# Cross-attention with a mixture of experts: GpSimd's large operations placed behind each tile's low part and doubled copy

## The reference, cut to what matters

```python
# 16 batch items: x (16, 56, 256), context (16, 1500, 256); 16 heads of 128
q = rms_norm(x @ q_w + q_b, nq_s)
k_img, v_img = rms_norm(img @ ki_w + ki_b, nki_s), img @ vi_w + vi_b    # first 257 context rows
k_txt, v_txt = rms_norm(txt @ k_w + k_b, nkt_s), txt @ v_w + v_b        # the other 1243 rows
out = sdpa(q, k_txt, v_txt) + sdpa(q, k_img, v_img)                     # scale 1/sqrt(128)
x = x + out @ o_w + o_b          # x is normalised before q
...
# then 32 experts of which each token takes 4, and a shared one
x = x + ffn(layernorm(x))
```

## Time and profile before

| | us |
|---|---|
| median of three runs | 1808.75 |
| the profiled execution | 1808.77 |
| its span, first to last instruction | 1807.0 |
| attention loop within it, about | 231 to 1364 |
| busy in the whole span: PE, DVE, POOL, ACT | 1718.9, 1343.6, 1199.1, 983.1 |

### The profile page before, as it was taken

The page is one execution under the profiler, slowest core; times in us unless marked ns, Lnnn a source line. Parts: engine busy times, 40 slices in busy tenths (PEclk is TensorE's granted clock), DMA queues, the critical chain, the costliest instruction groups (busy, mean ns, idle before and its releaser), DMA issues. The chain is left out here.

```text
span 1807.0 us, 31191 instructions
## 1 busy us (share of the span) xinstructions
PE 1718.9 (95%) x8731; PEld 1540.5 (85%) x8731; DVE 1343.6 (74%) x2561; ACT 983.1 (54%) x1657; POOL 1199.1 (66%) x1053
## 2 busy tenths in 40 slices
PE   7899989999999999999999999999996997699998
PEld 6677779989889889889899898898885896588887
DVE  4444577887878878878878878778775783677776
ACT  3455546665665665656665656656645662344443
POOL 1233578889888898898898898888866420233332
PEclk8999989999999999999999999999998997899999
DMA  3276574466565665665564665656566960233332
GB/s 116 91 251 230 203 200 109 113 129 125 133 123 123 135 128 119 137 137 124 129 132 120 128 128 131 122 124 134 116 196 185 326 210 28 97 113 114 116 115 71
DMA packets 419413, 251.25 MB, mean 139 GB/s; under 512 B 352320, under 2 KB 370880, under 8 KB 417568
## 3 DMA queue, kind: packets, MB, share of 16 engines
q1 hardware_dynamic: 419360, 250.61, 54.1%
HBM read 187.71 MB, written 60.10 MB: 137 GB/s over the span
## 5 line engine op out<-in xcount | busy, mean ns | idle before, releaser
L1405 ACT ACTIVATE p_high<-psum,key_rms 128x448 fp32r<-128x448 f32 x384 | 245.0, 638 | 345.9 <-PE psum L1226 345.8
L1224 PE MATMUL psum<-u_high,c_high 128*128 128x448 f32 x768 | 284.2, 370 | 6.5 <-POOLq L1837 5.9
L1224 PE MATMUL psum<-p_high,c_high 128*128 128x448 f32 (+1 forms) x768 | 284.8, 371 | 4.9 <-DVE p_low L1488 4.9
L1225 PE MATMUL psum<-u_low,c_high 128*128 128x448 f32 x768 | 281.9, 367 | 0.0
L1226 PE MATMUL psum<-u_high,c_low 128*128 128x448 f32 x768 | 281.6, 367 | 0.0
L1226 PE MATMUL psum<-p_high,c_low 128*128 128x448 f32 (+1 forms) x768 | 280.9, 366 | 0.0
L1225 PE MATMUL psum<-p_low,c_high 128*128 128x448 f32 (+1 forms) x768 | 280.9, 366 | 0.0
L1499 DVE COPY psum<-beta_wide 128x448 f32<-128x448 f32 x416 | 259.3, 627 | 20.2 <-DMA beta_wide<-absorbed_biases 4.4
L1488 DVE TENSOR_TENSOR p_low<-psum,p_high 128x448 fp32r<-128x448 f32 x384 | 236.7, 616 | 45.3 <-ACT psum L1407 42.9
L1719 POOL TENSOR_TENSOR c_low<-stage,c_high 128x512 fp32r<-128x512 f32 x208 | 270.3, 1300 | 0.0
L1407 ACT ACTIVATE psum<-psum,key_rms 128x448 f32<-128x448 f32 x384 | 232.9, 606 | 0.0
(11 more groups left out here) (274 smaller groups left out, 4032.6 us busy)
## 6 DMA issues: line engine op xcount, KB each, us to landing
stage<-in_ctx SPq DMA_DIRECT2D x210, 256.0 KB, 2.7
averages<-o_raw SPq DMA_DIRECT2D x64, 448.0 KB, 5.2
u_raw<-absorbed_queries SPq DMA_DIRECT2D x60, 448.0 KB, 5.5
absorbed_queries<-u_stage SPq DMA_DIRECT2D x14, 1792.0 KB, 6.8
u_stage<-averages SPq DMA_DIRECT2D x20, 896.0 KB, 6.1
beta_wide<-absorbed_biases SPq DMA_DIRECT2D x32, 448.0 KB, 5.4
recip_wide<-reciprocals SPq DMA_DIRECT2D x32, 448.0 KB, 4.0
p_wide<-probs_by_expert SPq DMA_DIRECT2D x32, 448.0 KB, 3.5
```

What stands on the lines that cost most here:

```text
L1224: nc.tensor.matmul(out, high, rhigh, start=start, stop=False, **kw)
L1225: nc.tensor.matmul(out, high, rlow, start=False, stop=False, **kw)
L1405: nc.scalar.activation(p_high[:, probs_slot(u), :], src, ACT.Exp, scale=key_rms[:, t:t + 1])
```

## The change

`X` moves from each even step to the odd step behind it, where it stands behind S and T. ACT's high parts of the image rows move from steps 10 and 12 to 11 and 13. `split_lone` moves from steps 17 and 19 to 16 and 18, so that it stands behind K. In the first item the scaling of the second text half stays at step 0. Every instruction is the same as before.

```diff
-        TEXT_SPLIT, IMAGE_SPLIT = (1, 3), (10, 12)
-        LONE_TERMS, LONE_HIGH, LONE_LOW = (12, 14), (14, 16), (17, 19)
+        TEXT_SPLIT, IMAGE_SPLIT = (1, 3), (11, 13)
+        LONE_TERMS, LONE_HIGH, LONE_LOW = (12, 14), (14, 16), (16, 18)
...
-                    if step == 0 and has_prev:
+                    if step == 1 and has_prev:
                         scale_u(it, TEXT, 1)
                     if step == 0 and not has_prev:
                         scale_first(TEXT, 1)
...
-                    if step in (2, 4):
-                        split_u(it, TEXT, (step - 2) // 2)
-                    if has_next and step in (8, 10):
-                        scale_u(it + 1, IMAGE, (step - 8) // 2)
-                    if has_next and step in (12, 14):
-                        split_u(it + 1, IMAGE, (step - 12) // 2)
-                    if has_prev and step in (16, 18):
-                        scale_o(it - 1, TEXT, (step - 16) // 2)
-                    if step in (20, 22):
-                        scale_o(it, IMAGE, (step - 20) // 2)
-                    if has_next and step == 24:
+                    if step in (3, 5):
+                        split_u(it, TEXT, (step - 3) // 2)
+                    if has_next and step in (9, 11):
+                        scale_u(it + 1, IMAGE, (step - 9) // 2)
+                    if has_next and step in (13, 15):
+                        split_u(it + 1, IMAGE, (step - 13) // 2)
+                    if has_prev and step in (17, 19):
+                        scale_o(it - 1, TEXT, (step - 17) // 2)
+                    if step in (21, 23):
+                        scale_o(it, IMAGE, (step - 21) // 2)
+                    if has_next and step == 25:
                         scale_u(it + 1, TEXT, 0)
```

## The result

The changed kernel takes 1811.13 us (median of 15 runs, 1807.16 to 1814.88) against 1807.43 for the kernel before (15 runs on the same chips, 1802.39 to 1809.63). The ratio is 1.0023, with a 95% interval of 1.0013 to 1.0033: slower by about the 0.2% that can be told from no change. The profiled execution has a span of 1809.4 us, against 1807.0.

A forecast was written before the change was run, and what follows sets the result against it. PE was taken as the bound, busy 69.67 of each item's 70.22 us. Items 2 to 16 +3.0, first item +1.3, last item -2.1 sum to +2.2 on 1808.75: forecast 1811.0 us, range 1803.5 to 1821.5.

The forecast's parts named there:

- The new wait at unit 7: PE waits about 1.1 us per item for the text rows' second low part, 5.33 after the norm of step 4.
- Rival 3: Change doesn't reach PE: text low part out in time, item stays 70.22, total 1808.8; chance 0.16.
- The held cast: DVE's row-sum cast beside step 1's text scaling on GpSimd ends 0.26 us after it; norm of step 2 only 0.95 earlier.
- Rival 2: Faster: DVE's cast is not held and the first item's clock stays up, -8.2 us, 1800.6; chance 0.14.
- rival 1: DVE's gain dies between the norms of steps 1 and 4; each item pays +0.76, total 1821; chance 0.25.
- PE's gains: Next item's first scores no longer wait, -0.31 us; the second lone unit's seed wait shrinks as DVE's norms come earlier.
- Per item: Unit 7 starts +0.12 to +0.26 us later, +0.20 taken; bounds -0.30 and +0.76; items 2 to 16 give +3.0.
- The last item: DVE's wait for a small DMA behind output loads ends 3 us earlier, PE gains 2.1 us; bounds -2.1 and 0.
- The first item: PE keeps 0.3 of 1.6 us gained; the clock's fall moves before unit 7, costing 1.6: +1.3 in all.
- The sum: Whole kernel: 3.0 + 1.3 - 2.1 = +2.2 us, forecast 1811.0.
- rival 4: The new gap drops PE's clock in each item: 15 x 1.6 us more, total 1835; chance 0.05.

The follow-up runs named there:

- e1: The changed kernel with the text rows' low parts back at steps 2 and 4, before the tile's low part; 1795.39 us, ratio 0.9935.
- e4: The changed kernel with step 1's text scaling done on half its columns, the rest left unscaled; 1797.06 us in one run.
- e7: The kernel before, order untouched, with the lone low parts computed for only 64 of 448 columns; 1793.29 us in one run.
- e6: The kernel before with only the image rows' scaling, low parts and ACT's high parts moved; 1795.37 us, ratio 0.9932.
- e3: e1 with the text scaling also back at steps 24 and 0, so no text operation is moved; 1792.99 us, ratio 0.9922.
- e8: e3 with the text low part's first half at step 3, behind the doubled copy, second half still at step 4; 1791.78 us, ratio 0.991.

## Why the prediction was right, and where it was not

**The new wait at unit 7: right.** 5.33 us from the norm of step 4 was forecast, 5.25 measured, and the wait is there in all 16 items: 1.01 beyond the pace in a steady one (1.1 forecast), 1.90 in the first. e1 prices it at 0.97 an item. Rival 3, a low part that is out in time, falls on it.

**The held cast: right in the full profile** (0.26 behind the scaling's end forecast, 0.25 measured), and e4 prices it at 0.62 of the item. Rival 2, faster because the cast is not held, falls on this row. So does rival 1, a cast held until DVE's whole gain is gone: its item would have been 0.76 longer, not 0.27.

**PE's gains: right in place.** The seed's wait and the hidden 0.31 at the item's first scores are gone. A hidden 0.22 at unit 5, where the forecast had a seed's wait shrink, stayed.

**Per item:** +0.20 forecast, +0.27 measured, just past the working's own 0.12 to 0.26 and well inside its outer bounds.

**The last item: right.** From its first lone matmul to its last attention matmul it took 65.12 and takes 63.19: -1.93 (-2.1 forecast). The wait for the sums' DMA fell from 4.77 to:
```profile
1324.08 0.20 DVE L1585 RECIPROCAL recip_cols<-sum_cols 112x8 f32<-112x8 f32 x1 [1.01 <-DMA sum_cols<-sums]
```

**The first item was mis-sized: +1.3 forecast, +0.5 measured** (72.84 to 73.34). The mechanism was right. PE now stands 1.90 later on, at 252.86, and the clock falls behind it instead of behind the earlier gap. Windows of the changed kernel (us, then busy and count for PE, PEld, DVE, ACT, POOL, then the granted clock, DMA share, GB/s):
```profile
249.00:250.00 1.00, 1.00 (x7) 0.92 (x6) 0.94 (x2) 0.55 (x2) 0.95 (x1) 1.00 1.03 414
...
253.00:254.00 1.00, 1.00 (x5) 0.90 (x6) 0.98 (x2) 0.00 (x0) 1.00 (x2) 0.77 0.30 99
254.00:255.00 1.00, 1.00 (x4) 0.92 (x3) 0.63 (x1) 0.05 (x1) 0.92 (x2) 0.50 0.03 10
```
The working charged the fall anew with 1.6 and gave only 0.3 back, although the same stretch of half speed (1.2 GHz) had already stood in the item before the change. It moved; it was not added. e7, whose first item has a gap of 0.66 in place of the 1.89 and no stretch at half speed, gives its price: the item is 2.74 shorter there, 1.23 of it by the gap, which leaves 1.5 for the clock. So the 1.6 was about the right size, but it was already in the 72.84.

**The sum.** To the output stage's first matmul (at 1370.33 before and 1373.98 now) the change costs 3.65: the prologue 0.6, the first item 0.5, fourteen items 4.46, the last -1.93. Of the fourteen, item 2 alone is 0.75 (69.73 to 70.48, below), the others 0.28 or 0.29 on the mean. Against the forecast's terms that is 0.6 and 1.46 more for the prologue and the items, 0.8 less for the first, 0.17 less given back in the last. The stages behind gave back 1.2, which no run explains, so the span grew by 2.4 against 2.2 forecast, and the median of many runs by 3.7. The near hit of the span is in part errors that cancel.

**What the reading missed,** though it did not spoil the sum, is what the stall was. The prediction took each wait of DVE's norm as the work of the X that stands in that pair. It was one lag: 0.86 were there when the averages' stretch began (e6 takes these away), two rounds that hold a lone low part and an averages' scaling made 1.60 of it, and it was carried over the item's end. The trace of before held the counterexample: item 1 has no text averages to scale at steps 16 and 18, its norms of the last steps have no wait,
```profile
279.90 0.43 DVE L1513 CUSTOM_DVE_ANT_0 junk<-psum,c_twice 128x257 bf16<-128x257 f32 x1 [0.56 <-POOL c_twice L1732]
...
284.85 0.43 DVE L1513 CUSTOM_DVE_ANT_0 junk<-psum,c_twice 128x257 bf16<-128x257 f32 x1
...
301.25 0.43 DVE L1513 CUSTOM_DVE_ANT_0 junk<-psum,c_twice 128x257 bf16<-128x257 f32 x1
```
and item 2 lasts 69.73 instead of 70.23, although its own text scaling stands before S as in every other item. Hence all of the change's gain (1.05 an item in e3) is to be had without the two moves that cost: text scaling, 0.35, and text low part, 0.97. 1.32 less 1.05 is the 0.27 of the changed kernel.

**Left open:** what the stages behind the loop gave back, and how much of the 0.6 in the prologue is chance: the starts of item 1's first lone matmul lie between 241.04 and 244.80 over the ten kernels, with no order in them that I can name.

## What to carry to other kernels

Where engines wait for each other in turn, measure the length of the round (norm to norm) against the pace of the engine that bounds the kernel. A round near that pace carries any lateness across many steps, and the place where the bound engine stalls is then not where the lateness arises. Move an operation behind the work that the round needs only if its own consumer lies farther away than the whole round, and if it doesn't land beside work of an engine that it can hold; here the last text low part failed the first condition and the text scaling the second. Compare an odd item out (the first, the second) with the steady ones before pricing a stall.

## What was not expected of the hardware

A DVE cast of 128x448 from SBUF is held until the GpSimd operation beside it ends. It takes 0.38 or 0.39 alone, and 1.07 or 1.70 beside a 2.13 us GpSimd operation, according to where in that operation it starts, ending 0.25 behind it in both cases (the changed kernel has 30 such casts in its attention stage, and all end 0.2 to 0.3 behind GpSimd's operation); a cast from PSUM beside such an operation (740.88, beside 740.63 to 742.76) kept its 0.62:
```profile
740.88 0.62 DVE L1540 CAST p_sum_high<-psum 128x448 fp32r<-128x448 f32 x1
```
A subtraction with both inputs in SBUF went from 0.62 to 1.05 (e3). GpSimd is slowed too, though by less: in e1 its low part took 1.44 instead of 1.29 beside such a subtraction (722.99, beside 722.65 to 723.27).

PE's clock stood at 1.00 in a whole item that holds a gap of about 1 us and is dense otherwise, and rival 4 fell with that; in the first item it fell to 0.50 behind a gap of 1.90. e7 and e8, where no gap in that place is longer than 0.66, kept 1.00 there: e7 in every window from 240 to 266, e8 in every one from 247 to 262.
